# Delta, B and C of a state-space scan from one product and a trip through DRAM, with re-spaced slots and filler products, in a two-layer image kernel on Trainium2

## The chip, the cores and the metric

One core of one Trainium2 chip runs the whole program in one launch. The metric is the time of that launch on the device, in microseconds (us), lower is better. All data of the scan is float32, and TensorE takes each float32 product as two instructions.

## The reference, cut to what matters

The input is 16 images of 48 channels, 64 by 64 pixels. Two layers follow each other; each is a mixer and a small feed-forward part (ffn) with quantized steps. The mixer of layer 0 is a 3 by 3 depthwise convolution with gelu and a pointwise convolution, whose weights a router chooses for each image. The mixer of layer 1 masks, transforms (DCT), normalizes and cuts the image into four quadrants of 1024 positions, and sends each through a mamba block, which is what the change touches:

```python
xi = silu(conv1d(in_w[:96] @ xs) + conv_b);  z = in_w[96:] @ xs
dt, Bm, Cm = split(xp_w @ xi)            # 6, 16 and 16 rows
delta = softplus(dt_w @ dt + dt_b)       # 96 rows
h_t = exp(delta_t * A) * h_(t-1) + delta_t * Bm_t * xi_t     # 96 x 16 states
y_t = sum_s(h_t * Cm_t) + xi_t * Dp;  out = out_w @ (y * silu(z))
```

## The kernel before, in words

The images are taken in 8 pairs, two images on 96 partitions (2 x 48 channels). Of each pair, layer 1 runs while the convolution of layer 0 of the next pair is slipped in between. A pair has about 175 us of transforms, normalization and ffn, and a scan stage of some 345 to 355 us. The change is all in the scan stage. The scan stage has 8 units (4 quadrants x 2 images) and each unit 12 steps (8 of the 96 channels with 16 states each, so 128 partitions, over 1024 positions). There are 768 steps in all.

**One step** (v is the unit, m the step). SyncE loads 8 rows of delta from DRAM, each copied to 16 partitions (`spread_delta`, L435, 512 KB, three buffers). ScalarE makes the decay, exp(A*delta) (L1167, three buffers). TensorE copies 8 rows of u = delta*xi to 128 partitions with a 0/1 matrix (`broadcast_u`, L796 and L798, which run side by side) into one of two PSUM double banks. VectorE multiplies by B (L1489) and scans (L1494, `h_ready`). GpSimd multiplies by C (L1582). TensorE sums the states, three steps at a time (`states`, L817). The broadcast of step m+2 needs the banks that scan m has read, so TensorE may run at most one step ahead of VectorE.

**The order on each engine** is written out by hand. `scan_stage` (L378) walks over unit and slot (a slot is a step's place in the unit) and calls in each slot `early`, `step`, `conv` and `prep`, of which the last prepares unit v+1. The constants at L55 to L64 say which slot each piece stands in. Before the change TensorE has, behind the broadcast of each slot:

- slot 0: `project_in`, both halves of xi (4 products, L699); 1: the last `states` of the unit before; 2: the gate z (2 products, L706); 3: `skip` (2, L809) and the delta product (2, L712); 4: `states`
- slots 5 to 9: the 9 taps of the convolution as 2, 2, 1, 2, 2 products (L864, bank 7), and with them in slots 5 and 6 half of B each, in slots 7 and 8 half of C each (`of_xi`, L712, on 96 x 128 weights `xp_rep` that copy each of the 16 rows to 8 partitions), with `states` in slots 7 and 10
- slots 9 and 10 of every second unit: the output product (L826, bank 6); 11: the pointwise product (L870, bank 7)

ScalarE copies B and C out of PSUM half by half (`keep_b` L1093, `keep_c` L1101), and has silu of xi (slot 1), copy of y (2, L1191), silu of z (3), softplus (4), the write of delta to DRAM (L1107, slot 6), the copy of u's rows to lower partitions (L1113, slot 8) and gelu (10), with a table load ahead of and behind each function that is no exp. Its copy of the pointwise product (`mix_bias`, slot 0) stands behind the decay of that slot. GpSimd makes u (slot 5), gates y (slot 1), and adds the convolution's result (slot 1). The last unit of a pair has nothing to prepare, and the last of the 8 pairs has no convolution.

**The first unit** is prepared ahead (`prep_first`, L715): TensorE waits for xs (`xs_in`), projects, then the delta product, B, the gate, and xi of the second unit. C of the first unit is made behind the first broadcast (`first`, L733). Its skip and the second unit's gate stand in slots 3 and 2.

## Time and profile before

| | us |
|---|---|
| median of 3 runs | 4353.88 (4338.94 to 4365.86) |
| the profiled execution's own time | 4352.36 |
| its span, first to last instruction | 4350.6 |
| mean granted clock of TensorE | 0.94 of full speed |

The span is what the trace shows; 1.8 us of the profiled execution lie around it. Busy time is summed for each engine, and the five engines run side by side. The profile's times of single instructions are that execution's.

### The profile page before, as it was taken

The numbers are of one execution on the slowest core, as the hardware profiler recorded it, in microseconds if no ns is written. First come the engines' busy times: TensorE is split into PE (matmuls) and PEld (weight loads), VectorE is DVE, ScalarE is ACT, GpSimd is POOL, SyncE is SP. The second block draws the span as 40 slices with busy tenths as digits, with TensorE's granted clock in tenths as the row PEclk, the third lists the DMA queues.
The fourth block names the chain that finished last, engine by engine and source line by source line (L and its number), as shares of the span: only waits on it lengthen the run. The fifth ranks groups of instructions, "written<-read, shape, count | busy, mean of one in ns | idle before, by whom it ended". The sixth has DMA issues, their size and how long they took to land.

```text
span 4350.6 us, 42094 instructions
## 1 busy us (share of the span) xinstructions
PE 3926.6 (90%) x14264; PEld 1447.7 (33%) x14264; DVE 3503.0 (81%) x3093; ACT 2822.8 (65%) x3380; POOL 2381.2 (55%) x1108
## 2 busy tenths in 40 slices
PE   6889997999879998799988999889998899978987
PEld 2332234322342223422244222432234322342223
DVE  1479977799668997699966998669987799667997
ACT  2567747677466775677666775767757677476764
POOL 0137752577426874177731787238752478425774
PEclk9989999899889999899998999989999899898888
DMA  1157751777417773377624775357751676406661
GB/s 41 45 125 193 176 135 45 171 175 187 99 53 181 182 180 89 80 181 183 169 61 114 184 183 133 88 124 182 183 139 47 155 187 179 109 21 165 159 176 46
DMA packets 166830, 578.92 MB, mean 133 GB/s; under 512 B 22572, under 2 KB 23416, under 8 KB 163064
## 3 DMA queue, kind: packets, MB, share of 16 engines
q1 hardware_dynamic: 152280, 538.47, 50.3%
q10 hardware_dynamic: 14336, 37.76, 2.9%
q8 instruction: 115, 1.88, 0.2%
q14 instruction: 99, 0.81, 0.1%
HBM read 466.93 MB, written 71.48 MB: 124 GB/s over the span
## 4 chain that ended last, share of the span: by engine, by line
PE 66%; DVE 16%; ACT 8%; issue 6%; DMA 2%; SPq 0%; POOL 0%; DVEq 0%; ACTq 0%; POOLq 0%
PE ps L796 15%; PE ps L864 10%; PE ps L817 9%; PE ps L712 6%; DVE arena L1494 6%; PE ps L699 5%; DVE ps L1489 4%; PE ps L626 4%; PE ps L566 3%; PE ps L809 3%; PE ps L706 3%; PE ps L617 3%; ACT arena L962 2%; ACT arena L944 2%; PE ps L645 1%
## 5 line engine op out<-in xcount | busy, mean ns | idle before, releaser
L1582 POOL TENSOR_TENSOR arena<-arena 128x1024 f32<-128x1024 f32 x768 | 1805.2, 2360 | 852.6 <-DVE arena L1494 852.6
L1494 DVE TENSOR_TENSOR_SCAN arena<-arena,ps 128x1024 f32<-128x1024 f32 x768 | 1756.3, 2287 | 35.9 <-ACT arena L1167 9.5
L1167 ACT ACTIVATE arena<-arena,a_all 128x1024 f32<-128x1024 f32 x768 | 866.3, 1141 | 323.2 <-DVE arena L1494 248.3
L1489 DVE TENSOR_TENSOR ps<-ps,arena 128x1024 f32<-128x1024 f32 x768 | 932.3, 1214 | 177.5 <-PE ps L798 176.2
L796 PE MATMUL ps<-arena,spread 32*128 32x512 f32 x1536 | 899.2, 666 | 98.5 <-DVE arena L1494 98.5
L798 PE MATMUL ps<-arena,spread 32*128 32x512 f32 x1536 | 899.3, 666 | 0.0
L817 PE MATMUL ps<-arena,gather 128*32 128x512 f32 x3072 | 529.6, 639 | 1.3 <-POOL arena L1582 1.3
L864 PE MATMUL ps<-x 96*96 96x512 f32 x1008 | 507.2, 621 | 0.0
L796 PEld LDWEIGHTS ps<-arena,spread 32*128 32x128 f32 x1536 | 233.3, 189 | 739.5 <-issue 437.2
L1543 POOL TENSOR_TENSOR x<-x,arena 96x512 f32<-96x512 f32 x64 | 113.3, 1771 | 371.9 <-DVE arena L1343 371.9
L919 ACT ACT_TABLE_LOAD x226 | 290.0, 1283 | 23.9 <-DMA wo<-in_wo 19.8
L699 PE MATMUL ps<-arena,w_in 96*96 96x512 f32 x512 | 263.3, 661 | 32.0 <-DMA arena<-xq 32.0
L712 PE MATMUL ps<-arena,xp_rep 96*128 96x512 f32 x512 | 263.3, 601 | 1.1 <-ACT arena L1093 1.1
L864 PEld LDWEIGHTS ps<-x 96*96 96x96 f32 x1008 | 142.9, 163 | 343.2 <-issue 343.2
L1101 ACT ACTIVATE arena<-ps 128x512 f32<-128x512 f32 x128 | 75.4, 595 | 280.1 <-PE ps L712 280.1
L566 PE MATMUL ps<-arena,average 96*96 96x512 f32 x400 | 221.3, 635 | 30.7 <-ACT arena L955 30.3
L798 PEld LDWEIGHTS ps<-arena,spread 32*128 32x128 f32 x1536 | 233.3, 189 | 0.0
L817 PEld LDWEIGHTS ps<-arena,gather 128*32 128x32 f32 x3072 | 106.7, 114 | 380.1 <-issue 315.8
L944 ACT ACTIVATE arena<-ps,eps 96x512 f32<-96x512 f32 x200 | 136.7, 683 | 143.0 <-PE ps L566 143.0
L1562 POOL MEMSET arena<- 96x6 f32 x8 | 0.8, 103 | 391.2 <-DVE xq L1466 391.2
L1312 DVE TENSOR_TENSOR arena<-ps,arena 96x512 fp8e5<-96x512 f32 x128 | 86.9, 679 | 127.8 <-ACT arena L949 127.8
L962 ACT ACTIVATE arena<-ps 128x1536 f16<-128x1536 f32 x128 | 183.7, 1435 | 1.6 <-PE ps L585 1.6
(155 smaller groups left out, 5128.3 us busy)
## 6 DMA issues: line engine op xcount, KB each, us to landing
arena<-dl SPq DMA_DIRECT2D x768, 512.0 KB, 5.4
dl<-arena ACTq DMA_DIRECT2D x64, 384.0 KB, 5.9
x<-pn SPq DMA_DIRECT2D x56, 247.5 KB, 7.0
arena<-in_x SPq DMA_DIRECT2D x9, 1536.0 KB, 16.7
arena<-xq SPq DMA_DIRECT2D x64, 192.0 KB, 5.8
arena<-arena ACTq DMA_DIRECT2D x64, 192.0 KB, 5.2
out<-x SPq DMA_DIRECT2D x64, 192.0 KB, 2.1
arena<-xq SPq DMA_DIRECT2D x64, 191.8 KB, 5.4
```

Source lines behind the costliest of these rows:

```text
L566: pe.matmul(ps[0:R, LN_DEPTH + j % LN_DEPTH, :], average[:], sq[:, j % LN_DEPTH, :], start=True, stop=True).then_inc(averaged, 1)
L699: mm = pe.matmul(ps[0:DI, 6 + c, :], w_in[:, q, j, :], xs[:, i, c * 512 + 2 * j:c * 512 + 2 * j + 512], start=(j == 0), stop=(j == 1))
L712: return pe.matmul(ps[0:rows, bank, :], weights, xi[:, i, c * 512:(c + 1) * 512], start=True, stop=True)
L796: pe.matmul(ps[:, bank, :], spread[rows[0], r, :], u[rows[0], i, 0:512], start=True, stop=True)
L798: pe.matmul(ps[:, bank + 1, :], spread[rows[1], r, :], u_low[rows[1], i, :], start=True, stop=True).then_inc(ubc_ready, 1)
L817: mm = pe.matmul(ps[b * BLK:(b + 1) * BLK, c, :], gather[:, r, :], hs[:, (r * TRIO + b) % HSS, c * 512:(c + 1) * 512], start=False, stop=( ...
L864: mm = pe.matmul(ps[0:R, 7, :], diag[:, k, :], taps_of(win[:, v % 2], k), start=(k == 0), stop=(k == TAPS - 1), skip_group_check=True)
L919: exp_table = lambda: act.preload_act_table_set("natural_log_exp_and_others")
L1167: act.activation(da[:, m % DAS, :], dbc[:, m % DBC, :], ACT.Exp, scale=a_all[:, v // 2, m:m + 1]).then_inc(da_ready, 1)
L1489: dve.tensor_tensor(driven, driven, bmat[:, v % 2, :], ALU.mult).then_inc(bu_ready, 1)
L1494: dve.tensor_tensor_scan(hs[:, m % HSS, :], da[:, m % DAS, :], driven, 0.0, ALU.mult, ALU.add).then_inc(h_ready, 1)
L1582: pool.tensor_tensor(product, product, cmat[:, v % 2, :], ALU.mult).then_inc(pr_ready, 1)
```

## The change

- **One product.** For units 1 to 7 of a pair the 96 columns of the delta weights and the 32 of B and C are one 96 x 128 weight `w_dbc`, so two products (slot 3) give delta on partitions 0 to 95 and B, C on 96 to 127. The four products of slots 5 to 8 go. ScalarE copies the 32 rows once (`keep_bc`, slot 4) and writes them to DRAM (`bc_to_rows`), SyncE loads B and C from there, each row copied to 8 partitions (`spread_b`, slot 8, `spread_c`, slot 9, 512 KB each). The first unit still makes B and C with the wide weights.
- **Evened slots.** `project_in` of the first half moves to slot 11 of the unit before (`PE_XI_EARLY`), the second stays in slot 0. The output products go from slots 9, 10 to 6, 8, their copies to 7, 9. The load of the convolution's window goes from slot 8 to 10.
- **Fillers.** `keep_warm` adds products with 32 columns of constants whose result nobody reads: 4 ahead of the wait for xs, 2 in slot 0 of the first unit.
- **Moves.** `mix_bias` stands in front of the decay of its slot. u is made in slot 4 (was 5), its rows are moved in slot 7 (8), delta is written in slot 4 (6). In the first unit the second unit's gate is in slot 1 (2), silu of it in slot 2 (3), the skip in slot 2 (3), and C behind the broadcast of slot 0.

```diff
-PE_DT, PE_B, PE_C, PE_OUT = 3, (5, 6), (7, 8), (9, 10)
-ACT_SILU, ACT_DL, ACT_U = 1, 6, 8
-ACT_DT, ACT_B, ACT_C, ACT_OUT = 4, (6, 7), (8, 9), (10, 11)
-POOL_U = 5
+PE_DBC, PE_OUT, PE_XI_EARLY = 3, (6, 8), 11
+ACT_SILU, ACT_ROWS, ACT_U = 1, 4, 7
+ACT_DBC, ACT_OUT = 4, (7, 9)
+POOL_U = 4
+SP_B, SP_C = 8, 9
+S_SKIP_FIRST, PE_Z_FIRST, ACT_SILU_Z_FIRST = 2, 1, 2
+WARM_XI, WARM_SCAN = 4, 2
-SP_STORE, SP_LOAD = 3, 8
+SP_STORE, SP_LOAD = 3, 10
...
+                def spread_state(v, k, dst, landed, freed):
+                    sync.wait_ge(bc_out, bc_count(p, v) * 16)
+                    if v >= 2:
+                        settled(sync)
+                        sync.wait_ge(freed, (p * UNITS + v - 1) * G)
+                    rows = slice(DI + k * NS, DI + (k + 1) * NS)
+                    sync.dma_start(dst[:, v % 2, :],
+                                   a["dl"][v % 2][rows, :].rearrange("(n o) t -> n o t", o=1)
+                                   .broadcast_to([NS, DG, L])).then_inc(landed[v % 2], 16)
...
+                def keep_warm(count):
+                    for _ in range(count):
+                        pe.matmul(ps[DI:128, 0, :], gather[:, 0, :], spread[:].rearrange("p r m -> p (r m)"),
+                                  start=True, stop=True, skip_group_check=True)
...
                 def prep_first():
                     V = p * UNITS
+                    keep_warm(WARM_XI)
                     pe.wait_ge(xs_in[0], (p * QUADS + 1) * XSL)
...
+                def states_first():
                     for c in range(2):
-                        of_xi(128, c, xp_rep[:, 0, 1, :], 0, c).then_inc(c_ps, 1)
+                        pe.wait_ge(xi_ready, 2 * (p * UNITS + 1) + c + 1)
+                        of_xi(128, 6 + c, xp_rep[:, 1, :], 0, c).then_inc(first_c_ps, 1)
+                    keep_warm(WARM_SCAN)
...
                     if slot == PE_XI and v >= 2:
-                        for c in range(2):
-                            if c and v >= 2 and not last:
-                                pe.wait_ge(pwb_ready, (p + 1) * NCH + v - 1)
-                            project_in(V, q, i, c)
+                        if not last:
+                            pe.wait_ge(pwb_ready, (p + 1) * NCH + v - 1)
+                        pe.wait_ge(bc_ready, bc_count(p, v - 1))
+                        project_in(V, q, i, 1)
+                    if slot == PE_XI_EARLY and v + 1 < UNITS:
+                        pe.wait_ge(xs_in[1 - i], (p * QUADS + (v + 1) // 2 + 1) * XSL)
+                        pe.wait_ge(bc_ready, bc_count(p, v))
...
+                        project_in(V + 1, (v + 1) // 2, 1 - i, 0)
...
-                    if slot == PE_DT:
+                    if slot == PE_DBC:
                         for c in range(2):
                             pe.wait_ge(sz_ready, 2 * V + c + 1)
-                            of_xi(DI, 6 + c, wdt_all[:, q, :], i, c).then_inc(dt_ready, 1)
+                            of_xi(128, 6 + c, w_dbc[:, q, :], i, c).then_inc(dt_ready, 1)
...
+                def keep_bc(v):
+                    act.wait_ge(dt_ready, 2 * (p * UNITS + v) + 2)
+                    if bc_count(p, v) > 1:
+                        act.wait_ge(bc_out, (bc_count(p, v) - 1) * 16)
+                    act.activation(bc, two(6)[DI:128], ACT.Copy).then_inc(bc_ready, 1)
...
+                def bc_to_rows(v):
+                    act.wait_ge(bc_ready, bc_count(p, v))
+                    act.dma_start(a["dl"][v % 2][DI:128], bc).then_inc(bc_out, 16)
...
-                    if slot == ACT_DT:
+                    if slot == ACT_DBC:
                         softplus(v)
+                        keep_bc(v)
                         exp_table()
```

The taps of slot 5 wait for `bc_ready` in place of `delta_ready`. VectorE's first step of a unit waits for B's load in place of `b_ready`, GpSimd's for C's.

## Rows read from the trace of the kernel before

**Rows 1.** The page: busy time, the chain that ended last, two DMA issues.

```profile
...
PE 3926.6 (90%) x14264; PEld 1447.7 (33%) x14264; DVE 3503.0 (81%) x3093; ACT 2822.8 (65%) x3380; POOL 2381.2 (55%) x1108
...
PE 66%; DVE 16%; ACT 8%; issue 6%; DMA 2%; SPq 0%; POOL 0%; DVEq 0%; ACTq 0%; POOLq 0%
...
arena<-dl SPq DMA_DIRECT2D x768, 512.0 KB, 5.4
dl<-arena ACTq DMA_DIRECT2D x64, 384.0 KB, 5.9
```

**Rows 2.** Stretches: busy by engine, granted clock, DMA share, GB/s.

```profile
core 0: us, PE busy (x) PEld busy (x) DVE busy (x) ACT busy (x) POOL busy (x), PEclk, DMA share, GB/s
1838.42:1885.85 47.43, 43.11 (x129) 12.33 (x125) 41.48 (x24) 29.41 (x32) 29.21 (x13) 0.86 0.78 189
1885.85:1928.37 42.52, 42.30 (x147) 12.47 (x145) 41.15 (x25) 31.58 (x35) 34.03 (x16) 1.00 0.72 183
1928.37:1971.93 43.56, 43.56 (x152) 12.81 (x152) 41.37 (x25) 32.65 (x36) 34.55 (x16) 1.00 0.73 181
1971.93:2015.12 43.19, 42.97 (x149) 12.52 (x145) 41.25 (x24) 32.04 (x35) 33.49 (x16) 1.00 0.74 186
2145.44:2185.77 40.33, 35.23 (x116) 8.85 (x112) 39.91 (x23) 15.66 (x15) 30.04 (x14) 0.87 0.43 109
1094.19:1142.20 48.01, 43.42 (x116) 10.49 (x112) 40.23 (x23) 15.66 (x15) 30.02 (x14) 0.72 0.38 92
4067.85:4111.84 43.99, 39.38 (x127) 10.68 (x125) 41.16 (x25) 28.16 (x30) 32.79 (x15) 0.85 0.72 173
```

**Rows 3.** Groups by line, whole execution: count, busy us, mean ns, idle before.

```profile
...
L1494 DVE TENSOR_TENSOR_SCAN arena<-arena,ps 128x1024 f32<-128x1024 f32 x768 | 1756.3, 2287 | 35.9 <-ACT arena L1167 9.5
L1489 DVE TENSOR_TENSOR ps<-ps,arena 128x1024 f32<-128x1024 f32 x768 | 932.3, 1214 | 177.5 <-PE ps L798 176.2
...
L796 PE MATMUL ps<-arena,spread 32*128 32x512 f32 x1536 | 899.2, 666 | 98.5 <-DVE arena L1494 98.5
...
L817 PE MATMUL ps<-arena,gather 128*32 128x512 f32 x3072 | 529.6, 639 | 1.3 <-POOL arena L1582 1.3
L864 PE MATMUL ps<-x 96*96 96x512 f32 x1008 | 507.2, 621 | 0.0
...
L712 PE MATMUL ps<-arena,xp_rep 96*128 96x512 f32 x512 | 263.3, 601 | 1.1 <-ACT arena L1093 1.1
...
L1191 ACT ACTIVATE arena<-ps 96x1024 f32<-96x1024 f32 x64 | 65.3, 1020 | 110.8 <-PE ps L817 110.3
```

**Rows 4.** Timeline of VectorE, first unit of the fourth pair.

```profile
...
1858.58 1.23 DVE L1489 TENSOR_TENSOR ps<-ps,arena 128x1024 f32<-128x1024 f32 x1 [3.02 <-PE ps L798]
```

**Rows 5.** Timeline of ScalarE in slot 4 of the third unit, fourth pair.

```profile
...
1944.12 1.26 ACT L1084 ACTIVATE arena<-ps,small_all 96x512 f32<-96x512 f32 x2
1945.40 1.28 ACT L919 ACT_TABLE_LOAD   x1
1946.69 2.19 ACT L1167 ACTIVATE arena<-arena,a_all 128x1024 f32<-128x1024 f32 x2
```

**Rows 6.** Timeline of VectorE beside it.

```profile
...
1945.60 2.29 DVE L1494 TENSOR_TENSOR_SCAN arena<-arena,ps 128x1024 f32<-128x1024 f32 x1
...
1949.04 2.29 DVE L1494 TENSOR_TENSOR_SCAN arena<-arena,ps 128x1024 f32<-128x1024 f32 x1
```

**Rows 7.** Stretches as above: a scan stage starts, low clock in a last unit.

```profile
1838.00:1849.00 11.00, 6.91 (x16) 1.93 (x16) 10.47 (x7) 6.26 (x8) 6.02 (x3) 0.69 1.04 236
1114.00:1128.00 14.00, 14.00 (x26) 3.31 (x25) 8.20 (x5) 3.24 (x3) 6.83 (x3) 0.50 0.32 75
```

**Rows 8.** Timeline of TensorE where the fourth scan stage is prepared.

```profile
...
1810.15 5.96 PE L617 MATMUL ps<-ident,arena 128*96 128x128 f32 x32 [5.23 <-DVE arena L1427]
1820.10 6.12 PE L699 MATMUL ps<-arena,w_in 96*96 96x512 f32 x8 [3.99 <-DMA arena<-xq]
```

**Rows 9.** Timeline of VectorE there.

```profile
...
1815.27 2.10 DVE L1466 TENSOR_SCALAR xq<-ps,ln_wb 96x512 f32<-96x512 f32 x2 [0.28 <-PE ps L617]
```

More of the change, by code:

```diff
@@ L186, in program @@
         cmat = two_of(cut(128, 2 * L))
-        delta = cut(DI, L)
+        delta_bc = cut(128, L)
+        delta, bc = delta_bc[0:DI], delta_bc[DI:128]
         u = two_of(cut(DI, 2 * L))
@@ L264, in program @@
         dt_ready = sem("dt_ready")
-        b_ps = sem("b_ps")
-        c_ps = sem("c_ps")
-        b_ready = sem("b_ready")
-        c_ready = sem("c_ready")
+        first_b_ps = sem("first_b_ps")
+        first_c_ps = sem("first_c_ps")
+        first_b = sem("first_b")
+        first_c = sem("first_c")
+        bc_ready = sem("bc_ready")
+        bc_out = sem("bc_out")
+        b_in = [sem("b_in0"), sem("b_in1")]
+        c_in = [sem("c_in0"), sem("c_in1")]
         delta_ready = sem("delta_ready")
@@ L457, in prep @@
                         shifted(v + 1)
+                    if v and slot == SP_B:
+                        spread_b(v)
+                    if v and slot == SP_C:
+                        spread_c(v)
                 def first():
@@ L757, in prep @@
-                    if slot == PE_Z:
+                        if not last:
[5 more added lines that the diff above has]
+                        pe.wait_ge(bc_ready, bc_count(p, v))
+                        if v >= 3 and i == 1:
+                            pe.wait_ge(mo_copied, 2 * (p * QUADS + (v - 1) // 2))
+                        project_in(V + 1, (v + 1) // 2, 1 - i, 0)
@@ L835, in step @@
                         broadcast_u(w, k)
-                    if m == S_SKIP:
+                    if v == 0 and m == 0:
+                        states_first()
+                    if m == (S_SKIP if v else S_SKIP_FIRST):
                         skip(v)
@@ L889, in final @@
                     project(QUADS - 1, 1, 7)
-                scan_stage(prep, first, step, conv, final)
+                scan_stage(prep, lambda: broadcast_u(0, 0), step, conv, final)
                 pe.wait_ge(mo_copied, (p + 1) * 2 * QUADS)
@@ L1119, in early @@
                         return
-                    if slot == ACT_SILU_Z:
+                    if slot == (ACT_SILU_Z if v >= 2 else ACT_SILU_Z_FIRST):
                         act.preload_act_table(ACT.Silu)
@@ L1155, in prep @@
                         exp_table()
-                    if slot == ACT_DL:
+                    if slot == ACT_ROWS:
                         delta_to_rows(v)
+                        bc_to_rows(v)
                     if slot == ACT_U:
@@ L1194, in step @@
                     w, k = after(v, m, DAS - 1)
+                    if m == ACT_PW and v and not last:
+                        mix_bias(v - 1)
                     if m == ACT_Y and v:
@@ L1220, in conv @@
                         exp_table()
-                    if slot == ACT_PW and v:
-                        mix_bias(v - 1)
                 def final():
@@ L1484, in step @@
                     n = V * G + m
-                    if m == 0:
-                        dve.wait_ge(b_ready, 2 * V + 2)
+                    if m == 0 and v:
+                        dve.wait_ge(b_in[v % 2], state_in(p, v))
+                    elif m == 0:
+                        dve.wait_ge(first_b, 2 * p + 2)
                     driven = two(2 + 2 * (m % 2))
@@ L1577, in step @@
                     n = V * G + m
-                    if m == 0:
-                        pool.wait_ge(c_ready, 2 * V + 2)
+                    if m == 0 and v:
+                        pool.wait_ge(c_in[v % 2], state_in(p, v))
+                    elif m == 0:
+                        pool.wait_ge(first_c, 2 * p + 2)
                     pool.wait_ge(h_ready, n + 1)
```

81 lines of the change are left out of this document (29 added, 52 removed).

## The prediction

> **What bounds the kernel now.** I read the page's busy times and chain first. TensorE is busy 90% and holds 66% of the chain that ended last, VectorE 16% [rows 1]. That is an average over two kinds of stage, so I went to the stretches of the scan stage, cut at the scan of each unit's first step [rows 2]. In the units 2 to 6 of a pair TensorE is busy for the whole unit, 43.56 us of 43.56 or 42.97 of 43.19, at the full clock, and VectorE for 41.3 of them. Then the groups: VectorE's two instructions take 1.21 and 2.29 us, and two scans in a row on the timeline give the pitch of an undisturbed step, 1949.04 - 1945.60 = 3.44 us [rows 3, 6]. Twelve are 41.3 us. So TensorE sets the middle units, at 43.4 us on average, and right behind it stands VectorE at 41.3. No more than the difference can be had while VectorE does the same work; its instructions aren't touched. All of VectorE's waiting for a broadcast is 176.2 us [rows 3].
>
> What each unit can give, in the fourth pair [rows 2]: the first 47.43 - 41.3 = 6.1; the second 42.52 - 41.3 = 1.2; the third to seventh 43.56, 43.19 and again 43.56, 43.20, 43.56, so 2.3 + 1.9 + 2.3 + 1.9 + 2.3 = 10.7. Sum 18.0 us a pair. The last unit (40.33, counted to the scan's end, so 11 x 3.44 + 2.29 = 40.1) has nothing left.
>
> **The one product.** It takes away 4 of the B and C products in each of 56 units (7 a pair). By the group one is 263.3 / 256 = 1.03 us [rows 3]. Priced like this (broadcast 899.2 / 768 = 1.17, a tap 507.2 / 504 = 1.01, one `states` 529.6 / 256 = 2.07), TensorE's list for a unit adds up to some 47.5 us, while at the full clock it takes 43.4; so at full clock everything is 0.91 of it: broadcast 1.07, a product 0.92, `states` 1.89. Without the four, TensorE's unit is 43.4 - 3.7 = 39.7, under VectorE's 41.3. The delta product grows from 96 to 128 columns; the B products have 128 and cost what the others do, so I add nothing.
>
> **The slots.** An average isn't enough, since TensorE may run behind VectorE only until a broadcast comes late: 3.44 less the broadcast's own 2 x 0.67 = 2.1 us [rows 3]. I add up, slot by slot, what it needs over 3.44. Before: slot 0 has 1.07 + 4 x 0.92 = 4.75 (1.3 behind), slots 1 and 2 win back 1.0, slot 3 adds 1.3 (1.6), slot 4 wins 0.5, slots 5 and 6 add 0.4 each (1.9), and slot 7 with `states`, a tap and half of C adds 1.3: 3.2, over 2.1, which is a stall. After: slots 0 to 2 need 2.9 to 3.0, slot 3 4.75 (1.3 behind), 4 and 5 win 1.0 back, 6 with an output product 3.9 (0.7), 7 3.9 (1.2), 8 with the other 3.9 (1.6), 9 and 10 win 1.0, 11 with the pointwise product and the early `project_in` 3.8 (1.0), and slots 0 and 1 clear that. The peak is 1.6 of 2.1. So the stalls of the second to seventh unit all go, 11.9 us a pair, in the seven pairs with a convolution.
>
> **The first unit.** Its loss is one place: the clock falls after two waits of TensorE for a scan, and the gate, skip and delta products run at half of it; VectorE waits 3.02 us for one broadcast there [rows 4], and the unit's mean clock is 0.86 [rows 2]. After the change the wait of slot 0 holds C's two products and two fillers (4 x 0.92 = 3.7 us), slots 1 and 2 two products each, and nothing is heavy until slot 3. I take the 6.1 us as won. If the clock still fell, about 4 of it would stay.
>
> **ScalarE.** It loses four copies and gets one of 32 rows by 1024. It isn't shown before; the copy of 96 by 1024 out of PSUM takes 1.02 us [rows 3], and the two copies of 512 that it replaces cannot be cheaper than it by more than half, so 0.5 to 1.1; I take 1.02, the same length of row. It stands between softplus and the table load of slot 4, where ScalarE is solid: the load ends at 1946.68, two decays follow, the first ending at 1947.83, and scan 6 starts at 1949.04 [rows 5, 6]. With 1.04 more that decay ends at 1948.87, 0.17 before it is needed. A pass, narrowly: 0 to 0.3 us a unit. I take 0.1, 5 us in all. The write of delta and the write of B and C that follow it in slot 4 are behind the decay. `mix_bias` ahead of its decay frees bank 7 a decay (1.1 us) sooner for `project_in`; the decay has two steps of room.
>
> **DMA.** B and C come to a unit 4 steps before they are used, 13.8 us, against 5.9 for the write and 5.4 for a load [rows 1]; the write is issued at the end of slot 4 and the loads behind it, so B waits for the write, not VectorE for B. SyncE's queue is in order: behind `spread_b` stands the delta load of the next unit's first step, which now waits for `bc_out` too; that one is issued some 7 us before its scan's decay has to start. The engines' load grows. A middle unit moves 182 GB/s x 43.4 us = 7.9 MB at a share of 0.73, 31.7 us of full use [rows 2]. Two loads of 0.52 MB at the 236 GB/s that a full share moved [rows 7] are 4.4 us, the write 0.6: 36.7 of 41.3 us, a share of 0.89. In slots 8 to 11 four delta loads, B, C and the window ask for some 3.6 MB in 13.8 us, more than 236 GB/s gives by 1.5 us, which three delta buffers hide. I take 0, with up to 1 us a unit (56 us) as the bad end.
> The Trainium skill (DMA: Bandwidth & Descriptors, section Where 436 GB/s comes from) gives a core about 358 GB/s from HBM. By that figure an estimate of the share would be 9.1 MB / 41.3 us / 358 = 0.62 and there would be no question here; the row of this case is tighter, and it decides.
>
> **The fillers ahead.** The wait for xs lasts 4.0 us, and then 8 instructions of `project_in` take 6.12 instead of 3.6, at the low clock [rows 8]. The fillers can start when the last evacuation is done, at 1815.27 + 2.10 = 1817.4 [rows 9], 2.7 us before xs is there, and need 3.7 at full clock, 7.4 at half. If they hold the clock, `project_in` starts 1.0 later and takes 2.5 less: 1.5 won. If not, it starts 4.7 late and wins nothing. That being busy alone doesn't bring the clock back, a row shows: 14 us with TensorE busy throughout, at 0.50 [rows 7]. The fillers are narrow, 32 columns. I take 1 us a pair lost, 8 in all, between 12 won and 38 lost.
>
> **The last unit and the last pair.** The last unit isn't changed. In 2 of the 7 pairs it took 48.0 instead of 40.3, at a mean clock of 0.72 [rows 2]; I expect as many again, and 0 to 5 would be -15 to +23 us. The last pair has no taps; its middle units take 41.4 or 44.0 at clocks of 0.85 and up [rows 2]. With B and C gone its TensorE has still less to do between heavy slots and will fall to the low clock as often. I take nothing for these, 6 us for its first unit.
>
> **The sum.** 7 x 18.0 = 126 won, 6 in the last pair, 1 from 0.3 MB less of constants; 5 for ScalarE and 8 for the fillers lost: 120 us. The profiled execution took 4352.4, of which 4350.6 is the span; 4352.4 - 120 = 4232. It stands 1.5 below the median of the runs, so the prediction is 4232, 2.8% faster.
>
> **The rivals.**
> - *Part of it is eaten by ScalarE or DMA.* For it: 0.17 us of room, a share of 0.89. Against: in the middle units nothing but TensorE made VectorE wait. With 0.5 to 1 us a unit the time is 4232 + 28 to 56 = 4260 to 4288. Chance 0.13.
> - *The clock falls in the middle units: slower.* TensorE gets 1.6 us of idleness a unit, in slots 0 to 2 and 9, 10. Where slots are thin now, in the last unit, the clock falls, and then `states` and taps run at half and TensorE has no reserve: 7.7 us (48.01 - 40.33). One fall a unit in the 42 middle units with taps would be 4232 + 323 = 4555. It decides from 120 / 7.7 = 16 falls on, when nothing is left. Against: each of these slots keeps 2.9 of 3.44 us of work, where the last unit's slots 0 and 2 have only a broadcast. Chance 0.05 for 16 or more, 0.06 for 7 to 15 (4286 to 4347).
> - *The change does less than it says*, since the low clock of the first unit stays and the fillers cost their worst: 4232 + 7 x 4 + 30 = 4290. Chance 0.06.
> - The forecast, 4205 to 4260: 0.70.
>
> **From this to the numbers.** The range 4200 to 4285 leaves out the clock rival, half of the third and a bit below. A measurement of this kernel tells about 1% from no change: 4310 and 4397. Below 4310 lie the forecast, the first and the third rival, 0.89, and a little of the clock's smaller case: 0.90; within 1% the rest of that: 0.05; the clock's larger case counts as slower: 0.05.
>
> **What would show it.** Right: middle units of 41.3 us; TensorE busy 39 to 40 of them, with idle time that scans end; the clock 1.00 there; no wait of VectorE in slots 8 to 10; a first unit near 41.5; DMA share near 0.9. Wrong: decays that end behind the multiplication in slots 5 to 7, or that wait for `dl` in slots 10 to 1; a clock under 1.00 in middle units; `project_in` starting more than 5 us behind the evacuations.

## The result and the profile after

The kernel after takes 4329.06 us, the median of eight runs (4312.02 to 4343.77), beside 4353.55 for eight runs of the kernel before on the same chip: the ratio is 0.9936, with a 95% interval of 0.9915 to 0.9958. That is 0.6% faster where 2.8% was forecast, and 44 us above the range. The profiled execution took 4330.65 us, 21.7 less than that of before. The ratios, here and below, leave out slow runs: one before (4675.23), and the one of 4296.59 among the four with the window's load in slot 2, whose median is 4238.75 without it.

The page of the kernel after, against [rows 1]:

```profile
...
PE 3795.6 (88%) x13912; PEld 1364.5 (32%) x13912; DVE 3489.6 (81%) x3093; ACT 2773.3 (64%) x3212; POOL 2378.9 (55%) x1108
...
DVE 28%; PE 26%; issue 21%; ACT 14%; DMA 6%; POOL 4%; SPq 0%; DVEq 0%; ACTq 0%; POOLq 0%
...
arena<-dl SPq DMA_DIRECT2D x880, 512.0 KB, 7.0
```

TensorE lost 131 us of busy time and its part of the chain fell from 66% to 26%: it is no longer what sets the end. But nothing else took its place as a clear bound (VectorE 28%, time in which the profile shows no releaser 21%, ScalarE 14%, DMA 6% where it was 2%). The loads of a B, C or delta block now land after 7.0 us, not 5.4.

Two groups of the page, of ScalarE's decays (L1200, L1167 before) and of VectorE's multiplication that waits for a broadcast (L1524, L1489 before, [rows 3]):

```profile
...
L1200 ACT ACTIVATE arena<-arena,a_all 128x1024 f32<-128x1024 f32 x768 | 868.0, 1144 | 802.7 <-DMA arena<-dl 669.8
L1524 DVE TENSOR_TENSOR ps<-ps,arena 128x1024 f32<-128x1024 f32 x768 | 929.6, 1210 | 152.3 <-PE ps L832 152.0
```

ScalarE stood idle 670 us ahead of decays, for delta loads (72 before). VectorE still waits 152 us for broadcasts, although TensorE has less to do. No instruction of the scan waited for the loads of B and C themselves. The stretches of the fourth pair, unit by unit, as in [rows 2]:

```profile
core 0: us, PE busy (x) PEld busy (x) DVE busy (x) ACT busy (x) POOL busy (x), PEclk, DMA share, GB/s
1827.51:1868.86 41.35, 37.71 (x125) 10.41 (x124) 40.93 (x24) 27.99 (x28) 29.24 (x13) 1.00 0.92 228
1868.86:1911.40 42.54, 38.24 (x135) 10.71 (x132) 40.94 (x25) 29.75 (x29) 33.97 (x16) 1.00 0.85 208
1911.40:1958.85 47.45, 46.16 (x146) 12.64 (x144) 41.26 (x25) 33.55 (x34) 34.02 (x16) 0.89 0.84 205
1958.85:2001.06 42.21, 38.73 (x134) 10.80 (x134) 40.93 (x24) 29.39 (x29) 33.95 (x16) 0.99 0.85 204
2001.06:2045.20 44.14, 43.32 (x148) 11.94 (x146) 41.04 (x24) 32.92 (x33) 33.96 (x16) 0.97 0.84 203
2045.20:2091.96 46.76, 45.04 (x142) 12.68 (x140) 41.15 (x25) 31.51 (x32) 34.02 (x16) 0.89 0.86 206
2091.96:2133.69 41.73, 39.86 (x144) 10.73 (x140) 40.93 (x25) 32.37 (x32) 33.99 (x16) 1.00 0.84 199
```

The first unit is what was forecast: 41.35 us at the full clock, where it was 47.43 at 0.86. (41.35 is VectorE's pace, twelve steps of 3.446.) The next six are not 41.35 but 41.7 to 47.5. The two worst have a mean clock of 0.89, where [rows 2] have 1.00. The DMA share is 0.84 to 0.86 in them, where it was 0.72 to 0.74.

Summed over the whole execution, with units cut at the scan of each first step, and the profiled spans of both kernels. "Best" is the last experiment below:

| us | before | after | forecast | change | best, change |
|---|---|---|---|---|---|
| eight first units | 380.8 | 331.4 | -49 | -49.5 | -44.7 |
| 42 middle units with taps | 1817.1 | 1856.4 | -78 | +39.3 | -80.2 |
| 6 middle units of the last pair | 257.0 | 267.8 | 0 | +10.8 | -7.6 |
| eight last units | 338.2 | 338.8 | 0 | +0.6 | -11.9 |
| seven gaps between scan stages | 1220.9 | 1199.3 | +8 | -21.6 | -16.4 |
| rest of the span | 336.5 | 335.1 | -1 | -1.4 | +0.1 |
| span | 4350.6 | 4328.8 | -120 | -21.7 | -160.7 |

So the miss sits in the middle units: 117 us in the 42 with taps, 11 in those of the last pair; the gaps came out 30 better. The last units say nothing on the change: nothing is changed in them, and over the executions of all the kernels here they sum to between 322.8 and 345.8. The third unit of the fourth pair (47.45 us) shows how. ScalarE on the timeline, from slot 10 of the unit before it:

```profile
...
1906.06 1.15 ACT L1200 ACTIVATE arena<-arena,a_all 128x1024 f32<-128x1024 f32 x1 [4.62 <-DMA arena<-dl]
...
1908.53 0.68 ACT L1253 ACTIVATE arena<-ps,sel_small 96x512 f32<-96x512 f32 x1
...
1915.15 1.15 ACT L1200 ACTIVATE arena<-arena,a_all 128x1024 f32<-128x1024 f32 x1 [2.90 <-DMA arena<-dl]
1917.08 1.15 ACT L1200 ACTIVATE arena<-arena,a_all 128x1024 f32<-128x1024 f32 x1 [0.78 <-DMA arena<-dl]
1918.24 1.28 ACT L1185 ACT_TABLE_LOAD   x1
1919.54 1.26 ACT L1096 ACTIVATE arena<-ps,small_all 96x512 f32<-96x512 f32 x2
```

TensorE beside it (of the products that broadcast, none is shown until 1922.84):

```profile
...
1909.26 1.10 PE L904 MATMUL ps<-arena,pw_gated 96*96 96x512 f32 x2 [1.19 <-ACT arena L1253]
...
1920.28 2.63 PE L743 MATMUL ps<-arena,w_in 96*96 96x512 f32 x4 [1.29 <-ACT arena L1096]
1922.84 1.22 PE L830 MATMUL ps<-arena,spread 32*128 32x512 f32 x1
...
1924.85 3.73 PE L841 MATMUL ps<-arena,dskip 96*96 96x512 f32 x4
1928.37 3.52 PE L749 MATMUL ps<-arena,w_dbc 96*128 96x512 f32 x4
```

VectorE:

```profile
...
1924.97 1.23 DVE L1524 TENSOR_TENSOR ps<-ps,arena 128x1024 f32<-128x1024 f32 x1 [0.95 <-PE ps L832]
```

And two stretches around it, columns as above:

```profile
...
1904.00:1908.00 4.00, 3.44 (x20) 0.72 (x16) 3.93 (x4) 1.92 (x2) 2.92 (x2) 1.00 1.03 249
1921.50:1931.00 9.50, 9.50 (x14) 2.81 (x12) 6.01 (x4) 9.29 (x10) 7.79 (x4) 0.50 0.39 90
```

The reader is to see a line of events. The DMA engines are full (a share of 1.00 to 1.06, at 223 to 265 GB/s, in each stretch of 4 us from 1892 to 1916). The decay at 1906.06 has waited 4.62 us for its delta. ScalarE works in order, so the table load and the gelu behind it wait too, and TensorE's pointwise product waits 1.19 us for the gelu. Two more decays wait 2.90 and 0.78 us in slots 0 and 1, and behind them stands the first silu; TensorE's gate waits 1.29 us for it. VectorE has not lost anything yet: decays and broadcasts run ahead of it. But now TensorE's clock falls: 0.50 from 1921.5 to 1931, while it is busy 9.50 us of 9.50. The gate takes 2.63 us, where its four instructions take 1.9 at the full clock, the broadcast 1.22 instead of 0.69, the skip 3.73 and the delta product 3.52. The next scans of VectorE start 4.5 and 8.0 us apart (1921.73, 1926.23, 1934.26) instead of 3.44. The unit ends 6.1 us over VectorE's 41.35.

The fall of the clock isn't the whole of it. The 42 middle units with taps lose 119.7 us against 41.35 each: 69 in the 16 of them with a mean clock under 1.00, 50 in the 26 that keep the full clock. And VectorE loses in two ways there, 76 us before multiplications, for a broadcast, and 38 us before the scan of step 6, for its decay (in 32 of the 42 units). The fourth unit of this pair shows the second, ScalarE first:

```profile
...
1979.15 3.23 ACT L1200 ACTIVATE arena<-arena,a_all 128x1024 f32<-128x1024 f32 x3
```

```profile
...
1980.38 2.29 DVE L1529 TENSOR_TENSOR_SCAN arena<-arena,ps 128x1024 f32<-128x1024 f32 x1 [0.90 <-DVE ps L1524]
```

The first of the three decays ends at 1980.30, and the scan starts behind it. (The profile names the multiplication, but that had been done for 0.90 us.) ScalarE was late since slots 0 to 3, and in slot 4 softplus, the copy of B and C and the table load stand ahead of this decay. The prediction gave it 0.17 us of room, and in the best version, where ScalarE isn't late, it ends 0.16 us before the scan of the fourth pair's third unit starts. So the copy fits, but leaves no room for any lateness.

TensorE's waits for ScalarE's two silus (of xi, L1096, and of the gate, L1106) and its gelu (L1253) over the whole execution (us in total, times, longest). They sum to 68.8 us; the kernel before has none of them, and in its scan waits only 1.1 us for ScalarE's copy of B:

```profile
...
PE ps L749 <- ACT arena L1106: 25.8, 29, 1.1
...
PE ps L904 <- ACT arena L1253: 22.9, 23, 2.0
...
PE ps L743 <- ACT arena L1096: 20.1, 25, 1.4
```

### The profile page after: what moved, and what is told of

Its sections match the earlier page's. It is cut to its first block, busy times and chain, and to the rows that moved or that the text cites. A ratio compares the mean times of both kernels' runs of the same rounds, so it can differ in the third digit from the quotient of the medians.

```text
span 4328.8 us, 41504 instructions
## 1 busy us (share of the span) xinstructions
PE 3795.6 (88%) x13912; PEld 1364.5 (32%) x13912; DVE 3489.6 (81%) x3093; ACT 2773.3 (64%) x3212; POOL 2378.9 (55%) x1108
## 2 busy tenths in 40 slices
DMA packets 186044, 644.71 MB, mean 149 GB/s; under 512 B 25660, under 2 KB 26600, under 8 KB 182280
## 4 chain that ended last, share of the span: by engine, by line
DVE 28%; PE 26%; issue 21%; ACT 14%; DMA 6%; POOL 4%; SPq 0%; DVEq 0%; ACTq 0%; POOLq 0%
DVE ps L1524 11%; DVE arena L1529 11%; DMA arena<-dl 5%; PE ps L663 4%; PE ps L830 3%; PE ps L603 3%; PE ps L849 2%; PE ps L654 2%; ACT arena L996 2%; PE ps L736 2%; POOL arena L1619 2%; ACT arena L978 2%; POOL arena L1628 2%; ACT arena L1200 2%; PE ps L682 1%
## 5 line engine op out<-in xcount | busy, mean ns | idle before, releaser
L1200 ACT ACTIVATE arena<-arena,a_all 128x1024 f32<-128x1024 f32 x768 | 868.0, 1144 | 802.7 <-DMA arena<-dl 669.8
L1524 DVE TENSOR_TENSOR ps<-ps,arena 128x1024 f32<-128x1024 f32 x768 | 929.6, 1210 | 152.3 <-PE ps L832 152.0
L849 PE MATMUL ps<-arena,gather 128*32 128x512 f32 x3072 | 550.6, 662 | 6.6 <-POOL arena L1619 6.6
L1628 POOL TENSOR_TENSOR arena<-arena 96x1024 f32<-96x1024 f32 x64 | 150.6, 2353 | 149.3 <-ACT arena L1224 149.3
L1578 POOL TENSOR_TENSOR x<-col_all,arena 96x512 f32<-96x512 f32 x64 | 104.2, 1628 | 143.9 <-DVE arena L1376 143.9
```

The lines of the kernel that those rows point to most:

```text
L849: mm = pe.matmul(ps[b * BLK:(b + 1) * BLK, c, :], gather[:, r, :], hs[:, (r * TRIO + b) % HSS, c * 512:(c + 1) * 512], start=False, stop=( ...
L1200: act.activation(da[:, m % DAS, :], dbc[:, m % DBC, :], ACT.Exp, scale=a_all[:, v // 2, m:m + 1]).then_inc(da_ready, 1)
L1524: dve.tensor_tensor(driven, driven, bmat[:, v % 2, :], ALU.mult).then_inc(bu_ready, 1)
```

## The experiments

Three theories stood at the start. A: the added loads make deltas late, the decays hold ScalarE's queue, and TensorE's clock makes the loss larger. B: the copy of B and C on ScalarE. C: TensorE is thin enough now for its clock to fall by itself. All times are medians with their spread; the interval is that of the ratio to the kernel before on the same chip.

**The added loads taken away.** 16 columns of 1024 for B and C from the fourth unit on, so nearly no bytes:

```diff
+                    cols = L if v < 3 and p == 0 else 16
-                    sync.dma_start(dst[:, v % 2, :],
+                    sync.dma_start(dst[:, v % 2, 0:cols],
...
```

> The changed kernel, but from the fourth unit on the loads of B and C bring 16 of the 1024 columns instead of all; the products with B and C are still made, on old values. Every instruction and wait stays, only some 1 MB of traffic a unit goes. Theory A (the loads of B and C and the window crowd the delta loads of slots 8 to 11 out, the decays come late, and the rest follows): in the changed kernel's trace the units 1 to 6 of a pair sum to 265.5 us on average where 6 x 41.3 = 248 are possible, so up to 17.5 x 8 = 140 us go: 4190 to 4225 us, middle units of 41.3 to 41.8, no wait of a decay for DMA over 1 us in them. Theory B (the 32-row copy in ScalarE's slot 4 is what makes the decays late) and theory C (TensorE's thinner slots let the clock fall, whatever the loads do): 4310 to 4340, units as in the changed kernel.

Measured: 4200.2 us (4189.85 to 4204.76), ratio 0.966 (0.963 to 0.968). All middle units but a few took 41.35 us (1739.8 in the 42 with taps, which is 41.42 each) at a clock of 1.00. The third unit of the fourth pair:

```profile
...
1865.82:1907.17 41.35, 40.19 (x144) 11.17 (x140) 40.93 (x24) 32.27 (x33) 34.00 (x16) 1.00 0.81 197
```

That is A: 129 us come back with the bytes, and with them only, since every instruction and every wait of SyncE stays. TensorE idles 1.2 us of this unit, as its thinner work lets it, and its clock stays up, which leaves nothing for C with these slots.

One part of the expectation failed: decays still wait for loads over 1 us, 110 times in the 42 middle units with taps, up to 4.4 us. In all they wait 363 us where it was 670, and it costs nothing. Where they wait makes the difference. The decays of steps 9 to 11 wait as long as in the kernel after (231 us for 221), those of steps 0 to 3 wait 101 us instead of 415, and TensorE's waits for silu, gate and gelu go from 68.8 to 2.1 us.

**The copy made thin as well.** The same loads, and the copy out of PSUM over 16 columns:

```diff
-                    act.activation(bc, two(6)[DI:128], ACT.Copy).then_inc(bc_ready, 1)
+                    cols = L if v < 3 and p == 0 else 16
+                    act.activation(bc[:, 0:cols], two(6)[DI:128, 0:cols], ACT.Copy).then_inc(bc_ready, 1)
```

> The changed kernel with the thin loads of B and C and also a thin copy: from the fourth unit on ScalarE takes 16 of 1024 columns of B and C out of PSUM. Against the thin loads alone (4200) it prices the copy in slot 4, 1.02 us. By my margin of 0.17 us it costs VectorE 0 to 0.3 us a unit: 0 to 15 us less, 4185 to 4200. If ScalarE were what holds the rest: 40 us less or more, under 4160.

Measured: 4194.25 us (4183.66 to 4204.46), 6 below the run above, with overlapping spreads. The copy costs 0 to 6 us where loads are in time. B is out as the cause by itself. A thin copy beside full loads was not run, so how much of the 38 us before step 6 it would have saved is open.

**A fourth delta buffer.** All loads as in the kernel after, but a delta may be fetched one step earlier:

```diff
-DBC = 3
+DBC = 4
-        dbc_in = [sem("dbc_in0"), sem("dbc_in1"), sem("dbc_in2")]
+        dbc_in = [sem(f"dbc_in{k}") for k in range(DBC)]
```

> The changed kernel with four buffers for the delta loads instead of three (the scan stage's part of the arena has 1112 columns free, one buffer takes 1024). Theory A with a burst as the cause: each delta load can be issued a step (3.44 us) earlier, which is more than the wait of most decays for DMA, so most of the 140 us go: 4200 to 4260. Theory A with the unit's whole traffic as the cause (share near 1 all the time): a deeper queue wins little, 4310 to 4330. Theories B and C: 4310 to 4340.

Measured: 4219.22 us (4207.26 to 4223.35), ratio 0.971 (0.968 to 0.974). The two groups:

```profile
...
L1200 ACT ACTIVATE arena<-arena,a_all 128x1024 f32<-128x1024 f32 x768 | 865.5, 1142 | 648.2 <-DVE arena L1529 510.5
...
L1524 DVE TENSOR_TENSOR ps<-ps,arena 128x1024 f32<-128x1024 f32 x768 | 927.7, 1208 | 52.7 <-PE ps L832 52.7
```

Most of the decays' idle time is now that of an engine that is ahead and waits for VectorE; for loads they wait 135 us. VectorE's wait for broadcasts went from 152 to 53 us, which is 99 of the 123 us by which the span shrank; its wait for decays before step 6 went from 38 to 17, which is another 21. The loads themselves land no earlier, after 8.3 us by the page (7.0 after, 5.4 before). So the bytes are not too many; they were asked for too late.

**A fourth buffer in the kernel before.** The same edit there:

> The kernel before with a fourth delta buffer and nothing else. Theory 'TensorE sets its middle units': the decays' waits for delta loads (72.5 us before) shrink, middle units stay at 43.2 us and the time at 4345 to 4360 us, ratio 0.998 to 1.002. Theory 'a fourth buffer is worth its 110 us in any version of this kernel': 4250 to 4320 us.

Measured: 4351.85 us (4340.26 to 4373.09), ratio 0.999 (0.997 to 1.001). The 42 middle units took 1817.1 us, the same as without it, though the decays waited 32 us for loads instead of 72. The buffer is worth 110 us only where the change has been made; it isn't a gain of its own.

**The loads added to the kernel before.** Two loads of 512 KB a unit into a spare tile, in slots 8 and 9. They wait for the write of delta, and each also waits until the one before it has landed, which those of the kernel after don't; SyncE issues the delta loads behind them. So this run doesn't price the bytes alone:

```diff
+                    if v and slot in (8, 9):
...
+                        sync.dma_start(spare,
+                                       a["dl"][v % 2][k * NS:(k + 1) * NS, :].rearrange("(n o) t -> n o t", o=1)
+                                       .broadcast_to([NS, DG, L])).then_inc(spare_in, 16)
```

> The kernel before with two loads more in each of 56 units, 512 KB each, in slots 8 and 9, of the same shape as those of B and C, from delta's rows into spare columns that nobody reads; the result is the reference's. It prices the traffic by itself, beside the window in slot 8. Theory A: TensorE's surplus work hides a part; the decays come late in slots 10 to 3 as in the changed kernel: 4400 to 4480. If the loads hurt only together with the one product's chain (delta, B, C written in slot 4): 4350 to 4370.

Measured: 4389.29 us (4381.92 to 4408.6), ratio 1.008 (1.006 to 1.011). They cost 33 us there, which lies between the two expectations. A reason for so little that was not tested: a unit of 43.4 us leaves three buffers 3 x 3.62 = 10.9 us from one decay to that of the same buffer, where 41.3 leaves 10.3. The decays' waits for loads rose from 72 to 201 us, and the middle units with taps from 1817.1 to 1866.1. The mechanism is of the same kind: the fifth unit of the fourth pair, 43.56 at 1.00 before, is here

```profile
...
2031.92:2081.74 49.82, 47.10 (x152) 13.24 (x152) 41.80 (x25) 34.85 (x37) 34.51 (x16) 0.93 0.80 194
```

and TensorE in it, where the second half of `project_in` waits:

```profile
...
2036.55 3.03 PE L712 MATMUL ps<-arena,w_in 96*96 96x512 f32 x4 [2.72 <-ACT x L1220]
```

What stands behind the late decay here is not silu or gelu but ScalarE's copy of the pointwise product (L1220, `mix_bias`), for which TensorE waits 22.4 us in all, and not at all in the kernel before. The kernel after has this copy ahead of its decay.

**The window's load moved earlier.** Slot 6 instead of 10, to thin the queue in slots 8 to 11:

```diff
-SP_STORE, SP_LOAD = 3, 10
+SP_STORE, SP_LOAD = 3, 6
```

> The changed kernel with the load of the convolution's window (440 KB) in slot 6, where the share of the DMA engines falls to 0.5, instead of slot 10, behind B and C. Theory A (a burst in slots 8 to 11): a fifth less in the burst, so the worst waits of a decay, 4.6 us, shorten by some 1.9 us and a third to a half of the 129 us that the loads of B and C cost come back: 4265 to 4300. If the number of buffers alone counts and not the burst's size: 4320 to 4335.

Measured: 4421.43 us (4407 to 4471), ratio 1.017 (1.010 to 1.024): 92 us worse than the kernel after, where a gain was expected. ScalarE and then TensorE at the end of the fourth pair's second unit:

```profile
...
1885.60 1.15 ACT L1200 ACTIVATE arena<-arena,a_all 128x1024 f32<-128x1024 f32 x1 [3.94 <-DMA arena<-dl]
...
1888.06 0.68 ACT L1253 ACTIVATE arena<-ps,sel_small 96x512 f32<-96x512 f32 x1
```

```profile
...
1888.80 2.02 PE L904 MATMUL ps<-arena,pw_gated 96*96 96x512 f32 x2 [1.03 <-ACT arena L1253]
1890.61 3.62 PE L736 MATMUL ps<-arena,w_in 96*96 96x512 f32 x4
...
1896.17 3.73 PE L736 MATMUL ps<-arena,w_in 96*96 96x512 f32 x4
```

```profile
...
1896.29 1.23 DVE L1524 TENSOR_TENSOR ps<-ps,arena 128x1024 f32<-128x1024 f32 x1 [2.90 <-PE ps L832]
```

The decay of slot 10 has waited 3.94 us, TensorE waits 1.03 us for the gelu behind it, and the clock falls right there: the pointwise product takes 2.02 us and each half of `project_in`, in slots 11 and 0, 3.6 to 3.7 instead of 1.9. VectorE lost 2.7 us a unit in step 1 alone, on average (0.45 in the kernel after). The decays' waits for loads were the same in all, 672 us for 670; what differs is what stands behind them: TensorE's waits for the gelu rose from 22.9 to 93.0 us, and its clock fell 28 times in the 42 middle units with taps, for 10 times in the kernel after. With a fourth buffer the same edit is harmless:

> Both: window in slot 6 and four delta buffers. With the four buffers the middle units are near their floor already, so the window's place wins 0 to 10 us more than the four buffers alone (4219): 4205 to 4222. Over 4230 would say that the window's place matters for another reason.

Measured: 4208.75 us (4194.61 to 4222.9), ratio 0.966 (0.962 to 0.970), 10 us better than four buffers alone, with overlapping spreads. The decays wait 301 us for loads here, for 135 with four buffers alone: again the sum of these waits says little of the time.

**The window's load out of the burst.** In slot 2 of its own unit, three slots ahead of the taps that need it:

```diff
-SP_STORE, SP_LOAD = 3, 10
+SP_STORE, SP_LOAD = 3, 2
-                    if not last and slot == SP_LOAD and v + 1 < UNITS:
-                        load_window(v + 1)
+                    if not last and slot == SP_LOAD and v:
+                        load_window(v)
```

> The kernel after, three delta buffers, with the load of the convolution's window moved out of slots 10 and 11, where it stands with the delta loads and B and C, to slot 2 of its own unit, where few loads are under way. Theory 'what counts is how many bytes are asked for between slots 8 and 1': the decays' waits for delta loads fall from 355 times and 670 us to under 450 us and the time to 4240 to 4300 us. Theory 'any load ahead of a delta load in the queue costs, wherever it stands': 4315 us or more, with the waits moved to slots 2 to 5.

Measured: 4244.98 us (4231.51 to 4296.59), ratio 0.973 (0.969 to 0.976): 84 us won with three buffers, and without one byte less. The decays' wait for loads was 545 us, above the 450 expected; it fell by less than the time did. So neither expectation fits whole: the time went with the bytes in the burst, the count of waits didn't. What went are TensorE's waits for the silu and the gate in slots 2 and 3 (45.9 us, now 0.7), and with them the 1.0 and 0.9 us a unit that VectorE had lost in steps 5 and 6. The wait for the gelu is still there, 28 times, and five units of the pairs with taps take 48 to 50 us. In the fourth pair's second, TensorE's clock falls right behind that wait:

```profile
...
1827.94 2.02 PE L904 MATMUL ps<-arena,pw_gated 96*96 96x512 f32 x2 [1.02 <-ACT arena L1253]
1829.75 3.62 PE L736 MATMUL ps<-arena,w_in 96*96 96x512 f32 x4
...
1835.31 3.73 PE L736 MATMUL ps<-arena,w_in 96*96 96x512 f32 x4
```

**The evened slots undone.** Four buffers, output products in slots 9 and 10 and both halves of `project_in` in slot 0, as before:

```diff
-PE_DBC, PE_OUT, PE_XI_EARLY = 3, (6, 8), 11
+PE_DBC, PE_OUT = 3, (9, 10)
-ACT_DBC, ACT_OUT = 4, (7, 9)
+ACT_DBC, ACT_OUT = 4, (10, 11)
...
```

> The kernel after with four delta buffers, but without the evened slots: the two output products stand in slots 9 and 10 again, their copies in 10 and 11, and both halves of project_in in slot 0, as before. Theory 'fewer products are what counts' (a running sum of what TensorE needs over 3.44 us a slot, with four products less, stays under the 2.1 us that it may run behind): within 0.4% of the kernel with four delta buffers and evened slots, 4205 to 4235 us. Theory 'the evening is needed': middle units lose 1 us or more each in slots 0 and 1, 4260 us or more, and in the trace VectorE waits for a broadcast in these slots.

Measured: 4262.97 us (4257.44 to 4276.73), ratio 0.978 (0.976 to 0.981), 44 us slower than with the evened slots (in the profiled executions 45.3 in the 42 middle units with taps, 1800.7 for 1755.4). The expectation that only the number of products counts fell. The third unit of its fourth pair, TensorE and VectorE:

```profile
...
1894.72 0.69 PE L828 MATMUL ps<-arena,spread 32*128 32x512 f32 x1 [1.20 <-DVE arena L1527]
...
1895.87 6.94 PE L736 MATMUL ps<-arena,w_in 96*96 96x512 f32 x8
```

```profile
...
1903.91 1.23 DVE L1522 TENSOR_TENSOR ps<-ps,arena 128x1024 f32<-128x1024 f32 x1 [2.35 <-PE ps L830]
```

TensorE waits 1.20 us for a scan ahead of the broadcast, and the four products of slot 0 behind it (eight instructions) take 6.94 us instead of 3.6. VectorE waits 2.35 us for what comes next. The third, fifth and seventh unit of this pair take 43.98 us each, the others 41.3 to 42.4:

```profile
...
1895.83:1939.81 43.98, 43.98 (x146) 12.34 (x144) 41.15 (x25) 32.50 (x33) 33.96 (x16) 0.92 0.89 227
```

The evening pays for what a fall does: eight instructions behind one wait, at half the clock, are more lateness than TensorE may run up. That at the full clock they would not be is by the running sum only.

This is theory C after all, with the old slots. The loads are no later than with four buffers alone (the decays wait 144 us for them, for 135), TensorE waits 1.9 us in all for silus and gelu, and what the fall follows is TensorE's own idle time, a wait for a scan (17 of its 21 waits of 1.0 us or more for a scan have a fall within the next 5 us). There are 24 falls in the 42 middle units with taps, and none with four buffers and evened slots.

**The first unit's parts in the kernel before**: gate, skip and C's products moved and the fillers added, nothing else:

> The kernel before with only the fillers and the first unit's moves (gate in slot 1, silu of it and skip in slot 2, C behind the broadcast of slot 0). If these parts act by themselves: in the changed kernel the first unit takes 41.3 instead of 47.5 (8 pairs, 49 us) and the stretch between two scan stages 171 instead of 174.5 (7 times, 24 us), so 4354 - 73 = 4281, and this would be faster than the changed kernel. If the first unit's win hangs on the merged product or the evened slots: 4330 to 4354.

Measured: 4293.68 us (4289.76 to 4306.39), ratio 0.988 (0.985 to 0.991). First units 334.9 us for 380.8, gaps 1205.0 for 1220.9, middle units unchanged (1817.1). These parts are worth 59 us by themselves, more than the whole change as it stands.

**The fillers alone taken away** from the kernel after:

```diff
-WARM_XI, WARM_SCAN = 4, 2
+WARM_XI, WARM_SCAN = 0, 0
```

> The changed kernel without fillers (both counts zero). If the fillers hold the clock: the stretch between the scan stages goes back to 174.5 (24 us) and the clock falls in the first unit, 1 to 5 us in each of 8: 4329 + 24 + 8 to 40 = 4361 to 4393. If they only fill time: 4320 to 4329.

Measured: 4350.55 us (4337 to 4361), ratio 0.999 (0.997 to 1.001), 21 us slower. The fourth pair's first unit, and two rows of TensorE in it:

```profile
...
1834.99:1882.05 47.06, 44.77 (x121) 12.17 (x120) 41.26 (x24) 29.06 (x29) 29.27 (x13) 0.78 0.93 213
```

```profile
...
1837.33 0.69 PE L830 MATMUL ps<-arena,spread 32*128 32x512 f32 x1 [2.29 <-DVE arena L1529]
...
1843.67 3.73 PE L841 MATMUL ps<-arena,dskip 96*96 96x512 f32 x4
```

Without fillers TensorE waits 2.29 us for the first scan, its clock falls, and everything is back: 47.06 us at 0.78, though the products of the first slots have been moved. First units cost 45.5 us more in all (376.9 for 331.4), gaps 12.7. Middle and last units took 50 us less, so the total shows little of it; why they did is open. Which of the two groups of fillers keeps the first unit's clock wasn't separated, and they don't always keep it: with four buffers, with the window in slot 2 and in the best version one first unit of eight still took 45.9 to 47.1 us.

**The best of them**: four delta buffers and the window's load in slot 2.

> The kernel after with four delta buffers and the window's load in slot 2 of its own unit. Theory 'with the fourth buffer the queue is no limit any more': as with four buffers alone, 4205 to 4225 us. Theory 'some of the burst is still paid for with four buffers' (decays still waited 135 us for loads there): 4195 to 4205 us, middle units at 41.4 us.

Measured: 4190.07 us (4187.13 to 4191.66), ratio 0.961 (0.959 to 0.963). It beats both kernels. Its third and fourth unit of the fourth pair, and its decays:

```profile
...
1857.27:1898.62 41.35, 40.18 (x144) 11.16 (x140) 40.93 (x24) 32.02 (x33) 33.99 (x16) 1.00 0.93 226
1898.62:1939.97 41.35, 39.93 (x141) 11.40 (x140) 40.93 (x24) 30.94 (x31) 33.98 (x16) 1.00 0.89 218
```

```profile
...
L1200 ACT ACTIVATE arena<-arena,a_all 128x1024 f32<-128x1024 f32 x768 | 865.4, 1143 | 636.7 <-DVE arena L1529 578.2
```

Each is 41.35 us, VectorE's pace, at a DMA share of 0.89 to 0.93, higher than in the kernel after. For loads its decays wait 56 us, and TensorE no longer waits for silu, gate or gelu at all. In the 42 middle units with taps only 0.2 us is left over 41.35 each.

## Why the prediction was wrong, and where it was right

**The step that failed** is the DMA's: "In slots 8 to 11 four delta loads, B, C and the window ask for some 3.6 MB in 13.8 us, more than 236 GB/s gives by 1.5 us, which three delta buffers hide. I take 0, with up to 1 us a unit (56 us) as the bad end." Its share was right: 0.89 was forecast, 0.84 to 0.86 came in the middle units, which took longer than forecast, and 0.89 and 0.93 in the best version, where they took 41.35. What was not worked out is how long three buffers can hide a load. A buffer is free when its decay ends, and its next delta must be there three steps later, 3 x 3.44 = 10.3 us, less the decay's own 1.15: 9.2 us for queueing and landing. Landing alone has a median of 7.0 us now, and the longest took 13.7 (8.9 before). The prediction held the excess of 1.5 us against none of these times. The loads cost 4329 - 4200 = 129 us, over twice the bad end; with a fourth buffer (12.6 us for the same way) most of that is back.

**Why the bad end was too small**: it priced lateness by itself. The runs show two steps behind it. ScalarE's queue is in order, so gelu and silu are late with the decay, and TensorE waits for them about 1 us. Behind some of these waits the clock falls, and the next heavy products take twice as long (69 of the 120 us that the middle units with taps lose stand in units with a low clock). The second path is ScalarE's own: the late silu makes slot 4 late, and the decay of step 6 with it (38 of the 120 us). VectorE's waits for broadcasts were 152 us with three buffers, 53 with four. The first rival (ScalarE or DMA eats a part, 4260 to 4288, 0.13) named the right resource with the wrong price. The second (the clock falls, 4286 to 4347 in its smaller case, 0.06) has the time that was measured but the wrong cause: it let the clock fall because slots are thin. With the evened slots thin work alone doesn't do it in middle units, as the run without the loads and the best version show, with no fall in theirs. With the old slots it does, 24 times. That the prediction's reason against this rival held is due to the evening.

With the DMA engines full, the stretches from 1892 to 1916 moved 223 to 265 GB/s. The Trainium skill (DMA: Bandwidth & Descriptors, section Where 436 GB/s comes from) puts a core's limit from HBM at about 358 GB/s. The trace doesn't bear that figure out for these loads: their engines were full well below it. By it, as an estimate, the 3.6 MB of the burst would take 10 us of the 13.8, and the burst would not have been seen at all.

**The one product and the slots: right.** In the best version, where loads are in time, the 42 middle units give 80.2 us for the 78 forecast (7 x 11.9 less 5 for ScalarE). The ledger of lateness (a peak of 1.6 of 2.1 us) fits that VectorE waits for no broadcast in these units, but it isn't the whole reason: it counts at the full clock, and with the old slots, where TensorE's waits end in a heavy slot, 44 us are lost.

**The first unit: right in size** (49.5 for 49), and partly for another reason than given. Of its two reasons "nothing is heavy until slot 3" doesn't carry it alone: without the fillers the unit takes 47.1 us for 47.6 before. The fillers without the moves were not run. The loss "if the clock still fell" is then 5.7 us, not 4.

**ScalarE: right by itself, wrong beside late loads.** The copy takes 1.02 us, as taken (a group of 56 with a mean of 1016 ns), and costs 0 to 6 us for the 5 forecast. But the forecast's own sign of being wrong, a decay that ends behind the multiplication in slots 5 to 7, came in 32 of the 42 middle units with taps.

**The fillers ahead: wrong in sign.** "I take 1 us a pair lost, 8 in all" was between ends of 12 won and 38 lost. The gaps gave 21.6 us, and without the fillers 12.7 of them are gone, which is the prediction's good end; why the gaps are 8.9 us shorter even so is open. TensorE where the fourth scan stage is prepared, against [rows 8]:

```profile
...
1808.15 3.59 PE L755 MATMUL ps<-spread,gather 128*32 128x512 f32 x8 [1.42 <-DVE xq L1499]
1811.68 3.68 PE L736 MATMUL ps<-arena,w_in 96*96 96x512 f32 x8
```

The four fillers (eight instructions in the trace) take 3.59 us, the full clock, and `project_in` 3.68 behind them for 6.12. It was so in all eight pairs, in each of the ten kernels here that have the fillers; in the four that haven't, `project_in` takes 5.4 to 6.5 us in every pair. I had argued from a stretch of 14 us, busy and at 0.50, that being busy doesn't bring the clock back [rows 7]. That may be; here the clock had not fallen yet (it is 1.00 from 1806 on), and with the fillers it stayed.

**The last unit and the last pair**: last units came out as before (+0.6); the last pair lost 10.8 us to the same late loads, and wins 7.6 in the best version. I had taken nothing for both.

## What to carry to other kernels

When an edit frees the engine that sets the pace, the pace quickens for everyone: give each load the time from the moment its buffer comes free to its use at the *new* pace, and hold that against the longest landing under the new load, not the bytes against the bandwidth. If it doesn't fit, a buffer more (here 4 KB a partition, 110 us) or a large load moved out of the burst (84 us) buys the gain back; before the edit the same buffer was worth nothing. A wait for a load isn't a loss by itself, though: 363 us of them cost nothing in the run with thin loads. So look at what stands behind the waiting instruction in its engine's queue. A unit with a wait of 1.0 to 1.2 us ahead of TensorE's heavy slots, and a fall of the clock behind it, took 2.6 us more (43.98, the old slots) to 7.3 more (48.68, the window in slot 2).

## What was not expected of the hardware

- The same load of 512 KB, moved 4 slots earlier, cost 92 us with three buffers and nothing with four; moved to where the queue is empty, it gave 84 back. The bytes were the same in all of them (644.71 MB over the execution).
- Loads landed later in faster kernels: a median of 7.0 us in the kernel after, 8.3 with four buffers, 7.8 in the best version. The median landing time says nothing on whether loads are late; who waits for them does.
- TensorE's granted clock fell to 0.50 after single waits of 1.0 to 1.3 us, and stayed there although TensorE was busy without a gap (1921.5 to 1931 in the kernel after). Most such waits went by without a fall: TensorE had waited 1.19 us before the pointwise product of 1909.26, which ran in 1.10. In the 42 middle units with taps the kernel after has 38 waits of 1.0 us or more, and 8 of them have a fall within the next 5 us; with thin loads, with four buffers and in the best version there are 0 to 3 such waits and no fall.
- Four fillers with only 32 columns kept the clock up for what followed, in 8 of 8 pairs of every kernel that has them.
- The same decay ends 0.16 us before its scan in the best version, and in the kernel after it kept the scan waiting up to 1.29 us, with the same instructions ahead of it in its slot.
